# Moving DMAs between two queues and changing the order of transfers in the start-up of an attention and mixture-of-experts layer

## The reference

```python
xn = layernorm(x)
out = x + local_attention(xn) + mixture_of_experts(xn)
# attention: 16 heads of 16, windows of 128 tokens with stride 64, all its windows softmaxed;
#            the first 512 rows of the windows laid end to end are kept (4 windows, 320 tokens per sequence)
# experts: 8 experts, the best 2 of each token by x @ gate_w.T, softmax over the two scores,
#          expert(x) = (silu(x @ w1) * (x @ w2)) @ w3, summed with the two shares
```

## Time and profile before

| | |
|---|---|
| median of 3 runs | 744.41 us (744.39 to 744.56) |
| the profiled execution's own time | 744.41 us |
| its span in the trace | 742.70 us |
| mean granted TensorE clock | 0.981 of 2.4 GHz |
| busy share of the span: PE, DVE, ACT, POOL | 89%, 77%, 68%, 40% |

### The profile page before, as it was taken

The page is one execution under the profiler, slowest core; times in us unless marked ns, Lnnn a source line. Parts: engine busy times, 40 slices in busy tenths (PEclk is TensorE's granted clock), DMA queues, the critical chain, the costliest instruction groups (busy, mean ns, idle before and its releaser), DMA issues.

```text
span 742.7 us, 17175 instructions
## 1 busy us (share of the span) xinstructions
PE 664.1 (89%) x5648; PEld 515.0 (69%) x5649; DVE 572.3 (77%) x907; ACT 505.2 (68%) x880; POOL 297.9 (40%) x329
## 2 busy tenths in 40 slices
PE   0877776969999999999999999999989898999984
PEld 0655564848888878787878787788767676766663
DVE  4869899867777877777777777777857879797883
ACT  4545496566766666676767676767657787888884
POOL 3000470114445444444444454445311335666653
PEclk9999898999999999999999999999999999999998
DMA  8894677641111111111111111111147696875830
GB/s 290 277 261 139 168 269 251 195 173 41 46 54 45 50 47 57 42 49 49 57 42 50 49 54 45 49 49 49 42 135 206 183 263 187 278 197 174 223 118 29
DMA packets 66303, 92.56 MB, mean 125 GB/s; under 512 B 6384, under 2 KB 53360, under 8 KB 66256
## 3 DMA queue, kind: packets, MB, share of 16 engines
q1 hardware_dynamic: 57824, 70.40, 31.8%
q0 software_dynamic: 6864, 18.75, 8.0%
q10 hardware_dynamic: 1568, 2.76, 1.1%
HBM read 59.06 MB, written 32.83 MB: 124 GB/s over the span
## 4 chain that ended last, share of the span: by engine, by line
PE 64%; DVE 14%; ACT 9%; issue 7%; DMA 3%; POOL 2%; ACTq 0%; POOLq 0%; DVEq 0%; SPq 0%
PE PS L1206 57%; PE PS L1450 4%; DVE SMALL L903 4%; ACT WORK L753 3%; DVE XN L1062 2%; PE PS L1428 2%; DVE WALL L897 2%; ACT QS L748 1%; DMA XN<-in_x 1%; DVE WORK L972 1%; DVE WORK L965 1%; DMA KS<-parts_scratch 1%; DVE WALL L921 1%; ACT WORK L691 1%; ACT SIDE L760 1%
## 5 line engine op out<-in xcount | busy, mean ns | idle before, releaser
L350 DVE TENSOR_TENSOR WS<-WALL,WS 128x1024 fp32r<-128x1024 f32 x144 | 176.4, 1226 | 89.2 <-ACT WS L829 88.1
L1206 PE MATMUL PS<-WS,XTS 128*128 128x512 f32 x852 | 234.2, 410 | 2.7 <-DVE XTS L897 1.5
L1206 PEld LDWEIGHTS PS<-WS,XTS 128*128 128x128 f32 x852 | 149.6, 189 | 47.1 <-DVE XTS L897 14.2
L829 ACT ACTIVATE WS<-WALL 128x1024 fp32r x144 | 152.2, 1058 | 39.2 <-issue 36.7
L1206 PE MATMUL PS<-WALL,WORK 128*128 x568 | 136.0, 382 | 0.8 <-ACT WORK L845 0.8
L1206 PEld LDWEIGHTS PS<-WALL,WORK 128*128 128x128 f32 x568 | 102.3, 190 | 12.6 <-issue 1.0
L633 POOL DMA_INDIRECT WORK<-xn_scratch,WORK x72 | 100.8, 1400 | 24.7 <-issue 21.6
L574 POOL TENSOR_TENSOR OTS<-SIDE,XN 128x256 f32<-128x256 f32 x32 | 24.2, 755 | 210.8 <-DVE XN L1062 138.8
L637 POOL DMA_INDIRECT ys_scratch<-SIDE,WORK x36 | 41.9, 1165 | 117.1 <-ACT SIDE L855 117.1
L903 DVE TENSOR_REDUCE SMALL<-PS 128x8 f32<-128x1024 f32 x64 | 77.5, 1210 | 13.2 <-PE PS L1206 13.0
L753 ACT ACTIVATE WORK<-PS 128x512 f32<-128x512 f32 x128 | 69.4, 595 | 22.0 <-PE PS L1206 18.9
(11 more groups left out here) (137 smaller groups left out, 999.4 us busy)
## 6 DMA issues: line engine op xcount, KB each, us to landing
WALL<-in_wexp SPq DMA_DIRECT2D x28, 384.0 KB, 7.3
WALL<-ys_scratch SPq DMA_DIRECT2D x16, 512.0 KB, 7.1
parts_scratch<-WORK SPq DMA_DIRECT2D x32, 240.0 KB, 2.4
QS<-parts_scratch SPq DMA_DIRECT2D x16, 480.0 KB, 4.7
XN<-in_x SPq DMA_DIRECT2D x4, 1024.0 KB, 12.1
xn_scratch<-XN SPq DMA_DIRECT2D x4, 1024.0 KB, 7.5
WALL<-in_x SPq DMA_DIRECT2D x8, 512.0 KB, 5.9
KS<-parts_scratch SPq DMA_DIRECT2D x16, 240.0 KB, 3.9
```

Source lines behind the costliest of these rows:

```text
L350: eng.tensor_tensor(out=WS[:, 1 - k, half, 1], in0=weights, in1=WS[:, 1 - k, half, 0].bitcast(F32), op=ALU.subtract).then_inc(low_ready[ha ...
L829: act.activation(WS[:, 1 - k, half, 0], weights, ACT.Copy).then_inc(high_ready[half], 1)
L1206: return pe.matmul(o, a, b, start=start, stop=stop)
```

## The change

Four places change. `FIRST_EXPERTS` goes from 1 to 2, so ACT issues expert 1's weights too, four DMAs ahead of its copy of pair 3. In SP's start-up `store_xt(1)` now stands between `store_xn(0)` and `store_xn(1)`, and `store_xt(2)` between `outs(0, 1)` and `backs(0, 0, 0)`. After `begin(0)` SP issues experts 2 and 3, waits for `early_done`, issues experts 4 and 5, and then `load_tokens(1)`; before, it issued experts 1 and 2, then `load_tokens(1)`, then experts 3 to 5.

```diff
-FIRST_EXPERTS = 1
+FIRST_EXPERTS = 2
...
             store_xn(0)
+            store_xt(1)
             store_xn(1)
             outs(0, 0)
             outs(0, 1)
+            store_xt(2)
             backs(0, 0, 0)
             backs(0, 0, 1)
-            store_xt(1)
-            store_xt(2)
             store_xt(3)
...
             begin(0)
-            load_experts(FIRST_EXPERTS, EARLY - 1)
+            load_experts(FIRST_EXPERTS, EARLY)
             sp.wait_ge(early_done, 1)
+            load_experts(EARLY, LATE)
             load_tokens(1)
-            load_experts(EARLY - 1, LATE)
             begin(1)
```

## The result

The changed kernel takes 755.66 us (median of 4 runs, 754.35 to 756.56) against 744.48 us of the kernel before in the same comparison (744.39 to 745.72): ratio 1.0142, 95% interval 1.0124 to 1.0162. It is slower by 11.2 us; 6.5 were forecast, and the time lies above the stated range. The profiled execution took 756.35 us, with a span of 754.6 us.

The account below looks back on a forecast made before the run. The prediction took the start-up to be bound by PE and ACT handing tile pairs to each other, the stacks having 5.5 us to spare. Late stacks 5.3 plus clock 1.2 on 744.41 gave 750.9 us, range 746.6 to 753.4.

Parts of the forecast that it names:

- The wait ahead of store_xn(1): SP's start-up: store_xt(1) waits for four ACT copies, holding all behind it; store_xt(1) at 37.75, parts from 38.8 us.
- Expert 1 on ACT: ACT's start-up: four issues put copy 3 1.6 us later, the PE/ACT loop 1.2 to 1.6; hidden by late stacks.
- When the stacks land: Start-up, ahead of PE's first scores: 22.4 us of queued bytes, stacks at 59.0 with semaphore, +5.3 us (+3.3 to +7.3).
- The clock: PE's first scores: half speed after a pause of 4 us, three groups at +0.41 each, +1.2 us (0 to 2).
- Experts 2 to 5 ahead of load_tokens(1): Step to sequence 1: tokens land at about 109.8, hidden by ACT's projection at 111.09; 0 us (-0.2 to +2).
- rival with late tokens: Step to sequence 1: tokens landing at 112 to 113 cost 1 to 2 us on top, 752.4 us; chance 0.09.
- The covered steps: After the stacks: probabilities' buffer covered, load_tokens(0) covered by 2 us, later stores by 1 to 2 us; no cost.
- The faster rival: DVE, 104 to 120 us: weight traffic slows tag operations; removing it wins 1.2 us, 743.2 us; chance 0.03.
- The sum: Whole kernel: 5.3 + 1.2 = 6.5 us of delay at 60 us, nothing behind taking it back; 750.9 us.

Follow-up runs that it names:

- e5: Kernel before with one added wait: SP waits for the fourth copy ahead of store_xn(1), no transfer moved; 747.83 us against 745.09, ratio 1.0039.
- e15: The changed kernel, unaltered, profiled once more for scatter; 23.3 to 24.2 us not repeated exactly: 23.6 us from issue of store_xt(1) to PE's first scores.
- e18: Changed kernel with SP waiting for the stacks before store_xt(3), profiled a third time; 23.2 us from issue of store_xt(1) to PE's first scores.
- e4: Changed kernel with load_tokens(1) ahead of experts 4 and 5; 754.27 us against 745.53 of the kernel before, ratio 1.0119.
- e9: Changed kernel with SP waiting for the stacks of sequence 0 before issuing store_xt(3) and what follows; 754.06 us against 745.03 of the kernel before, ratio 1.0117.
- e17: Changed kernel with SP waiting for the stacks before store_xt(3), profiled once more; 22.9 us from issue of store_xt(1) to PE's first scores.
- e2: Changed kernel with SP's start-up order undone, everything else changed; 747.82 us against 745.53 of the kernel before, ratio 1.0033.
- e7: Changed kernel with 48 extra unused transposes on PE ahead of its wait for the stacks; 753.91 us against 745.09 of the kernel before, ratio 1.0128.
- e8: Changed kernel with the old start-up order and load_tokens(1) behind 12 weight DMAs, not 16; 745.91 us against 745.09 of the kernel before, ratio 1.0008.
- e3: Kernel before with only expert 1's weights moved to ACT's queue (FIRST_EXPERTS = 2); 746.41 us against 745.53, ratio 1.0014.

## Why the prediction was wrong, point by point

- *The wait ahead of store_xn(1)*: right. The standstill, its end (36.5; 37.75 were forecast) and the parts at 37.8 (38.8 forecast) are in SP's queue. In the seven other profiles with this order and expert 1 on ACT it ended at 36.2 to 38.4. e5 shows that the wait alone makes the stacks late.
- *Expert 1 on ACT*: right in kind. Its four issues took 1.8 us and the copy of pair 3 moved by 0.4 us, not 1.6. The loop of PE and ACT ended no later than before in this execution (last products at 53.5), and it was covered by the stacks as forecast. That was luck of the execution: in e15 to e18 and e4 the same loop brought PE to its wait at 54.5 to 55.7, where 54.9 to 55.3 were forecast.
- *When the stacks land*: mechanism right, size short. 5.3 us were forecast, 7.0 measured, although SP's standstill ended 1.2 us sooner than forecast. From the issue of store_xt(1) to the first scores the account has 59.0 - 37.75 = 21.25 us; the eight profiles of this order have 22.6 to 24.2. The mis-sized term is the end of it: the account let all engines finish together and put the semaphore 0.1 us behind them, and e9 has 2.0 us there. The bytes themselves took 0.6 us less than forecast in e9. So e9 is 1.4 us over the account and the changed kernel 2.9; of the difference between the two (24.2 - 22.6 = 1.6 us), the scatter of one execution (up to 1.3 us among the five) is as likely a part as any delay by later transfers. That S0 of e9 (58.83) meets the forecast 59.0 is luck: it started 1.5 us sooner. The Trainium skill ("DMA: Bandwidth & Descriptors", section "Latency and other measured facts") puts about 2 us of fixed cost on a DMA, most of it the receipt from the target memory. The traces don't show a receipt of that length: between the last data and the release there are 0.4 to 0.6 us (e9, e17, e18 for the stacks, e2 and the changed kernel for the tokens), and the rest of the 2 us is data still moving on few engines.
- *The clock*: right at this pause, 1.2 forecast and 1.2 measured (5.92 - 4.70), and e7 shows it by removing it. Leaving the ramp out would have been wrong here, since it falls on a chain of short groups.
- *Experts 2 to 5 ahead of load_tokens(1)*: this step failed. "So I take 0" stands in the prediction; 2.6 us were measured, and e2, e4 and e8 show it three ways. The bytes were forecast well. In the changed kernel 16 full engines would have been done at about 116 + 0.56 x 2 = 117.1, which is 108.9 in the old time scale (8.2 us of delay subtracted), where the forecast had weights until 108.5 and tokens behind them:

```profile
114.00:116.00 2.00, 1.00 1.04 404
116.00:118.00 2.00, 1.00 0.56 212
...
117.00:118.80 1.80, 1.00 0.13 51
118.80:119.40 0.60, 1.00 0.00 0
```

  but the semaphore came at 119.3, 2.2 us behind that, where I had allowed 0.5; as with the stacks, few engines (share 0.13) worked on until 118.8. In the old scale the tokens landed at 111.1, not 109.8. ACT in time, then DVE, show who could not absorb it:

```profile
121.96 0.53 ACT L691 ACTIVATE WORK<-PS,SMALL 128x320 bf16<-128x320 f32 x1 [3.29 <-PE PS L1206]
```

```profile
122.58 0.55 DVE L965 SCALAR_TENSOR_TENSOR WORK<-PS,SMALL,WORK 128x320 f32<-128x320 f32 x1 [2.98 <-ACT WORK L691]
...
127.86 1.16 DVE L897 TENSOR_TENSOR XN<-WALL 128x576 bf16<-128x576 bf16 x1
```

  PE projects, ACT takes the result (L691), DVE splits it (L965). DVE stood still for 2.98 us; before, it had no gap here:

```profile
111.77 0.54 DVE L965 SCALAR_TENSOR_TENSOR WORK<-PS,SMALL,WORK 128x320 f32<-128x320 f32 x1
```

  Two errors make it up. The landing is one. The other is the clock: PE came back at half speed after a pause of 3.9 us, and its four products took 2.50 us in place of 1.24. Had they taken 1.24, ACT would have had its input 1.3 us earlier, and DVE would have waited 1.7; had the tokens landed at 109.8 as well, 0.4. So 1.3 us are the clock's and 1.3 the later landing's; this split is worked out from the rows and was not measured by itself. What it rests on holds in all eight profiles with a wait for the tokens: the four products took 1.57 to 2.50 us there, and PL came 7.4 us behind their end each time, so landing and products count one for one. The clock's part differs between executions; in e2, where the products took 1.80, it is 0.6. The prediction counted the fallen clock at the first pause and forgot it at the second. Its own sum left no room: 109.8 + 1.2 = 111.0 against ACT at 111.09. Its rival with late tokens was the right one, but had the cost begin at a landing at 111 and put 1 to 2 us on 112 to 113; a landing at 111.1 cost 2.6.
- *The covered steps* (later stores, load_tokens(0), probabilities' buffer): right; no engine waited for them. *The faster rival* falls by a row: the slow tag operation at 127.86 above takes 1.16 us, as one did before. DVE's busy time in the stretches around the two is the same, in the changed kernel with no DMA traffic and in the kernel before under full traffic:

```profile
127.80:129.00 1.20, 1.17 (x3) 1.00 0.00 0
```

```profile
117.00:118.20 1.20, 1.17 (x3) 1.00 1.02 402
```

- *The sum*: 5.3 + 1.2 + 0 forecast; 7.0 + 1.2 + 2.6 measured, and 1.2 in the rest of the span on top, which I take for scatter.

## What to carry to other kernels

Before a store is moved ahead in a queue, look at what it waits for: everything behind it inherits that wait, and a transfer with 5.5 us to spare was late after a standstill of 6. When a transfer's landing behind a backlog is worked out from bytes, don't stop where 16 full engines would be done: the semaphore came 2.0 and 2.2 us later here, because the engines finish one after the other. Take that distance from a landing of the same kernel. And where a wait is added in front of the matrix engine, price the half clock behind it each time it occurs.

## What the runs showed of the hardware that was not expected

Early in the start-up the same products ran at two speeds although the granted clock reads 1.00 for the whole stretch, and the moment of the step differed between executions. First the kernel before, then the changed one (least, median and most ns of one, first and last start):

```profile
L1206 PE MATMUL PS<-WALL,WQKV x16: 432/727/870, 24.0 to 30.6; 128*128 128x320 f32 x16
```

```profile
L1206 PE MATMUL PS<-WALL,WQKV x16: 432/433/870, 24.0 to 29.7; 128*128 128x320 f32 x16
```

870 to 432 ns is a factor of two, so it looks like the two clock levels, before the trace has a first record of them; that is argued and not shown. It moved the next products by 0.85 us (30.83 and 29.98), and that is probably why the loop that ACT's four issues delayed still ended in time. The other profiles with expert 1 on ACT agree. Where the median product took 433 ns (the changed kernel, e2, e7, e8, e9), PE was through with the loop at 53.5 to 54.2; where it took 702 to 741 ns (e3, e4, e15 to e18), at 54.5 to 56.6.
